# Attention with 32 batches on one core: the context block turned by the vector engine from a second, block-arranged load, instead of by eight transpositions of the tensor engine

## The reference, cut to what matters

```
q  = einsum('oc,bcn->bon', Wq, layernorm(x))        # 512 x 1024 for each batch
k, v = split(einsum('oc,bcn->bon', Wkv, context))   # 512 x 1024 each
q  = softmax(q, over the 64 of a head) * scale
k  = softmax(k, over n)
ctx = einsum('bhdn,bhen->bhde', k, v)               # sum over the 1024 positions n
out = einsum('bhde,bhdn->bhen', ctx, q)
out = Wout @ out + b_out; normalised over its 128 rows; times g
x  = x + out
```

## Time and profile before

| | us |
|---|---|
| median of three runs | 1996.38 |
| the profiled execution | 1997.54 |
| its span | 1995.7 |
| PE busy in the span | 1921.1 (96%) |
| DVE busy | 1381.4 (69%) |
| ACT busy | 1039.4 (52%) |
| POOL busy | 804.2 (40%) |

### The profile page before, as it was taken

How to read it: one execution, slowest core, us unless ns; L and a number is a source line. 1 busy time by engine, 2 the same in 40 slices (tenths; PEclk the granted TensorE clock), 3 DMA queues, 4 the chain that set the end, 5 groups by cost and what they waited for, 6 DMA issues and landing times. The chain is left out here.

```text
span 1995.7 us, 29856 instructions
## 1 busy us (share of the span) xinstructions
PE 1921.1 (96%) x10780; PEld 1662.6 (83%) x10780; DVE 1381.4 (69%) x1985; ACT 1039.4 (52%) x1303; POOL 804.2 (40%) x456
## 2 busy tenths in 40 slices
PE   5999999999999999999998699999999999999999
PEld 4888888888888887878786689999999999999998
DVE  6888888888888888888885744444444455444443
ACT  4787878787878787878785611111111111111111
POOL 4767676767667676767673000000000000000000
PEclk9999999999999999999999799999999999999999
DMA  3111111121212111111111711111111111111110
GB/s 117 54 64 64 63 63 67 59 74 53 74 53 74 53 74 53 74 53 74 53 43 37 221 53 64 64 63 49 46 63 63 63 63 63 63 63 53 44 39 32
DMA packets 43999, 127.64 MB, mean 64 GB/s; under 512 B 4224, under 2 KB 14080, under 8 KB 43968
## 3 DMA queue, kind: packets, MB, share of 16 engines
q1 hardware_dynamic: 39360, 110.44, 15.9%
q0 software_dynamic: 4608, 16.78, 2.7%
HBM read 93.65 MB, written 33.55 MB: 64 GB/s over the span
## 5 line engine op out<-in xcount | busy, mean ns | idle before, releaser
L282 POOL TENSOR_TENSOR kT_lo<-kT,kT_hi 128x1024 fp32r<-128x1024 f32 x128 | 304.6, 2404 | 0.6 <-ACT kT_hi L329 0.5
L278 POOL TENSOR_TENSOR eq<-eq,q_inv 128x1024 f32<-128x1024 f32 x128 | 242.6, 1906 | 140.7 <-DVE q_inv L504 140.7
L966 POOL TENSOR_TENSOR rstd_c<-var_c,minus_half 128x8 f32<-128x8 f32 x32 | 52.8, 1649 | 549.5 <-DVE var_c L1105 549.5
L52 PE MATMUL ps<-w_ra_hi,xT_hi 128*128 128x384 f32 (+1 forms) x768 | 257.3, 335 | 0.0
L54 PE MATMUL ps<-w_ra_hi,xT_lo 128*128 128x384 f32 (+1 forms) x768 | 251.8, 328 | 0.0
L53 PE MATMUL ps<-w_ra_lo,xT_hi 128*128 128x384 f32 (+1 forms) x768 | 251.2, 327 | 0.0
L988 ACT CAST hT_hi<-ps 128x512 fp32r<-128x512 f32 x64 | 37.7, 589 | 375.1 <-PE ps L1162 375.1
L52 PE MATMUL ps<-w_b_hi,hT_hi 128*128 128x512 f32 x512 | 205.4, 401 | 0.0
L347 ACT ACTIVATE ek<-ps,k_min 128x1024 f32<-128x1024 f32 x128 | 142.7, 1114 | 119.6 <-DVE k_min L508 119.5
L54 PE MATMUL ps<-w_b_hi,hT_lo 128*128 128x512 f32 x512 | 200.8, 392 | 0.0
L53 PE MATMUL ps<-w_b_lo,hT_hi 128*128 128x512 f32 x512 | 200.3, 391 | 0.0
(11 more groups left out here) (142 smaller groups left out, 4577.2 us busy)
## 6 DMA issues: line engine op xcount, KB each, us to landing
x_sb<-in_x SPq DMA_DIRECT2D x64, 512.0 KB, 4.1
ctx_hi<-in_ctx POOLq DMA_DIRECT2D x32, 512.0 KB, 3.6
ctx_sb<-in_ctx SPq DMA_DIRECT2D x32, 512.0 KB, 3.3
attention_out<-o_sb SPq DMA_DIRECT2D x32, 512.0 KB, 2.6
o_sb<-attention_out SPq DMA_DIRECT2D x32, 512.0 KB, 3.9
out<-out_sb SPq DMA_DIRECT2D x32, 512.0 KB, 2.9
x<-in_L_ffn_A SPq DMA_DIRECT2D x2, 512.0 KB, 4.0
o_sb<-in_L_ffn_A SPq DMA_DIRECT2D x2, 512.0 KB, 3.7
```

Of the source, the lines that this page charges most:

```text
L52: pe.matmul(out, stat_hi, mov_hi, start=first, stop=False)
L278: pool.tensor_tensor(v, v, per_row(q_inv[:, i, :], 2 * HEADS, DH), ALU.mult).then_inc(q_normed, 1)
L282: pool.tensor_tensor(kT_lo[:, i % 2, :, :], kT[:, i % 2, :, :], kT_hi[:, i % 2, :, :].bitcast(F32), ALU.subtract).then_inc(kT_lo_ready, 1)
```

## The change

The context is read from memory a second time, in sixteen transfers for each batch, into a tile `ctx_blk` whose 32-wide column blocks are arranged so that transposing each 32 x 32 block in place gives the whole transposed context. Each transfer carries a block of 32 rows of the context, of which it takes every fourth run of 32 columns: 32 x 8 runs of 128 bytes. The sixteen stand on SP behind the load of x, and wait until DVE has turned the batch before. DVE transposes all 32 x 32 blocks with one instruction into a tile `cT` in SBUF (no longer in PSUM), between `query_lo(1)` and `max_queries(3)`. ACT's `cT_hi` copy reads `cT` and moves forward, from behind `exp_keys(3)` to before `norm_x`. `cT_lo` moves from DVE to POOL, between `norm_queries` 1 and 2. PE loses its eight transpositions; `RING` loses `C0`, so KT1 of the next step now follows QT2 in its slot. The load of `ctx_sb` no longer waits for the turned context.

```diff
-        "QT0", "K2", "M0", "QT1", "Q3", "QT2", "K3", "QT3", "C0"]
+        "QT0", "K2", "M0", "QT1", "Q3", "QT2", "K3", "QT3"]
...
             def load_context(b, p):
                 wait_for(sp, ctx_lo_ready, b - 1)
-                wait_for(sp, c_turned, b - 1)
                 sp.dma_start(ctx_sb[:, p, :], context[b]).then_inc(ctx_loaded[p], 16)
+
+            def load_blocks(b, p):
+
+                wait_for(sp, c_turned, b)
+                for q in range(P // 32):
+                    dst = ctx_blk[32 * q:32 * q + 32, :].rearrange("p (m c j) -> p m c j", m=NCH, j=32)
+                    for c in range(P // 32):
+                        src = context[b][32 * c:32 * c + 32, :].rearrange("i (m q j) -> i m q j", m=NCH, j=32)
+                        sp.dma_start(dst[:, :, c, :], src[:, :, q, :]).then_inc(blk_loaded[p], 16)
...
+            def context_turned_lo(b):
+                pool.wait_ge(cT_hi_ready, b + 1)
+                pool.tensor_tensor(cT_lo[:, :, :].rearrange("p a b -> p (a b)"), cT[:, :],
+                                   cT_hi[:, :, :].rearrange("p a b -> p (a b)").bitcast(F32),
+                                   ALU.subtract).then_inc(cT_lo_ready, 1)
...
-                act.copy(cT_hi[:, :, :].rearrange("p a b -> p (a b)"), flat("C0")).then_inc(cT_hi_ready, 1)
+                act.copy(cT_hi[:, :, :].rearrange("p a b -> p (a b)"), cT[:, :]).then_inc(cT_hi_ready, 1)
...
+            def turn_context(b, p):
+                dve.wait_ge(blk_loaded[p], 16 * 8 * (b - p) + 256)
+                wait_for(dve, cT_lo_ready, b)
+                dve.transpose(cT[:, :], ctx_blk[:, :]).then_inc(c_turned, 1)
...
-            def turn_context(s, par, edge):
-                wait_slot(pe, "C0", s, edge)
-                pe.wait_ge(ctx_loaded[par], 8 * (s - par) + 16)
-                out = flat("C0")
-                for n in range(NCH):
-                    last = pe.transpose(out[:, n * P:(n + 1) * P], ctx_sb[:, par, n * P:(n + 1) * P], ident[:, :])
-                last.then_inc(c_turned, 1)
```

More of the change, by code:

```diff
@@ L71 @@
 RING = ["KT0", "Q0", "KT1", "K0", "KT2", "Q1", "KT3", "K1", "Q2",
-        "QT0", "K2", "M0", "QT1", "Q3", "QT2", "K3", "QT3", "C0"]
+        "QT0", "K2", "M0", "QT1", "Q3", "QT2", "K3", "QT3"]
 SLOTS = 3
 DELAY = {"X": -1, "K": 0, "C": 0, "Q": 0, "KT": 1, "M": 1, "QT": 1, "O": 2}
-PER_BATCH = {"K": 4, "C": 1, "Q": 4, "KT": 4, "M": 1, "QT": 4}
+PER_BATCH = {"K": 4, "Q": 4, "KT": 4, "M": 1, "QT": 4}
 FIRST_STEP, FULL_FROM, FULL_TO, STEPS = -1, 4, BATCHES - 2, BATCHES + 2
@@ L93, in attention @@
         ctx_sb = sb("ctx_sb", [P, 2, N])
+        ctx_blk = sb("ctx_blk", [P, N])
+        cT = sb("cT", [P, N])
         ctx_hi = sb("ctx_hi", [P, 2, N], F32R)
@@ L140, in attention @@
         ctx_loaded = [sem(f"ctx_loaded{i}") for i in range(2)]
+        blk_loaded = [sem(f"blk_loaded{i}") for i in range(2)]
         x_loaded = [sem(f"x_loaded{i}") for i in range(2)]
@@ L164, in attention @@
         rstd_ready, xn_lo_ready = sem("rstd_ready"), sem("xn_lo_ready")
-        slot_read = {"K": k_exp, "C": cT_lo_ready, "Q": q_shifted, "KT": kT_copied, "M": m_lo_ready,
+        slot_read = {"K": k_exp, "Q": q_shifted, "KT": kT_copied, "M": m_lo_ready,
                      "QT": q_lo_ready}
@@ L190, in wait_slot @@
                 if n < 0:
-                    n, back = n + len(RING), back + 1
+                    n, back = max(m for m in range(len(RING)) if (m - n) % SLOTS == 0), back + 1
                 kind, i = RING[n][:-1], int(RING[n][-1])
@@ L242, in step @@
                     sp.dma_start(o_sb[:, 0, :], o_dram[0]).then_inc(shared["o_loaded"][0], 16)
+                if on("C", s, edge):
+                    load_blocks(s, par)
                 if on("O", s, edge):
@@ L306, in step @@
                     norm_queries(s, par, 1)
+                if C:
+                    context_turned_lo(s)
+                if Q:
                     norm_queries(s, par, 2)
@@ L432, in step @@
                     query_hi(s - 1, 1 - par, 2)
+                if C:
+                    context_turned_hi(s)
                 if X_:
@@ L439, in step @@
                     exp_keys(s, par, 3)
-                if C:
-                    context_turned_hi(s)
                 if Q:
@@ L597, in step @@
                     query_lo(s - 1, 1 - par, 1)
+                if C:
+                    turn_context(s, par)
                 if Q:
@@ L610, in step @@
                     invert_sums(s, 1)
-                if C:
-                    context_turned_lo(s)
                 if Q:
@@ L775, in step @@
                     turn_query(s, par, 3, edge)
-                if C:
-                    turn_context(s, par, edge)
                 if QT:
```

## The result

The changed kernel takes 2087.86 us, the median of four runs (2086.69 to 2090.23), against 1997.27 us for the kernel before, the median of four (1995.07 to 1999.42). The ratio is 1.0455, with a 95% interval of 1.0437 to 1.0473: 4.5% slower. The forecast was 2085, range 2050 to 2132, slower at 0.93.

A forecast was written before the change was run, and what follows sets the result against it. PE was taken as the bound, with a DVE-POOL-PE ring only 0.8 us shorter; 1.13 + 2.38 - 0.75 gave 2.76 us a step, 31 rounds 85.6, with the ends 88, so 2085 us, range 2050 to 2132.

The forecast's parts named there:

- The ring: DVE to POOL to PE and back to `m_lo`: 32.99 us a step, forecast to grow 2.76 to 35.75 us.
- to the start of POOL's first scaling: DVE from `m_lo` through the reciprocal, then handover to POOL: the transposition in this gapless stretch adds 1.13 us.
- POOL's dense stretch: POOL from its first query scaling to the last `kT_lo`, 15.06 us: the inserted `cT_lo` adds its full 2.38 us.
- slack before `add_weighted(3)`: PE's product needing POOL's last `kT_lo`: 0.80 us slack, of which 0.75 is usable and gets used up.
- from there to `m_lo`: From PE's last weighted product through T, folding and ACT to the next `m_lo`: 5.88 us, no addition forecast.
- the first and last rounds: Pipeline ends: the last round pays 0.75 us more, the first pass an estimated 2 us.
- the 0.79 us: PE's eight context transpositions per batch: 25.3 us in all, a gain only while PE binds, otherwise lost in idle time.
- the rival at 1971: Whole attention step: PE stays the bound and its removed transpositions save 25.3 us; chance 0.06.
- PE starts ... without idle time before it: At `add_weighted(3)`, PE's product needing the last `kT_lo`: starts at 621.84 without idling, read as 0.80 us slack.
- Adds nothing to it: ACT's forward copy, 1.0 us later through `exp_keys(3)`: splits PE's waiting, adds none, since the reciprocal moves 1.13 us.
- the estimate of 33 us: Second load's sixteen transfers a batch, if their constants of about 2.0 us added up; issues 0.53 us apart favoured overlap.
- The clock: Rival: PE's granted clock drops for about 3 us of work a step, costing 1.5 us, total 2131; chance 0.07.

The follow-up runs named there:

- e1: The changed kernel with POOL's `cT_lo` subtraction moved before `x_lo`, into idle time; 2031.35 us, ratio 1.0169 to the kernel before.
- e2: The changed kernel with DVE's transposition moved before `folded_lo`, where DVE waits for ACT; 2061.46 us, ratio 1.0322 to the kernel before.
- e6: The changed kernel with PE's eight context transpositions put back into slot `C0`, read by nobody; 2087.59 us, ratio 1.0447 to the kernel before.
- e4: The changed kernel with DVE's transposition, POOL's subtraction and ACT's `cT_hi` copy all moved into idle time; 1996.38 us, ratio 0.9997 to the kernel before.
- e3: The changed kernel with both DVE's transposition and POOL's subtraction moved into idle time; 2031.35 us, ratio 1.0169 to the kernel before.
- e5: The changed kernel without the second load, DVE transposing blocks of `ctx_sb` instead (output not the reference's); 2087.60 us, ratio 1.0448 to the kernel before.

## Why the prediction was right

**The ring.** Its four terms, with forecast and measured change in us: to the start of POOL's first scaling, +1.13 and +1.12 (11.25 to 12.37); POOL's dense stretch, +2.38 and +2.32 (15.06 to 17.38); slack before `add_weighted(3)`, -0.75 and -0.75 (0.80 to 0.05); from there to `m_lo`, 0 and +0.16 (5.88 to 6.04). The sum is 2.85 where 2.76 was forecast, on 32.99. 31 x 2.85 = 88.4 of the 90.9 us between the two profiled executions; 2.5 are left for the first and last rounds, 2.75 were forecast. That these two agree is luck: the first `m_lo` comes 1.44 us later (68.02 against 66.58), where 2 were estimated from no row, and the last round is 4.94 us longer (36.67 against 31.73), where 2.76 + 0.75 were forecast; the granted clock was 0.91 in it. Behind the last `m_lo` 907.0 us follow, against 907.3 before: the expert part is unchanged. e1 and e2 show that both pieces cost by their position: moved into idle time, POOL's gives back 56.5 us and DVE's 26.4.

**PE.** That the 0.79 us lie in idle time was right (e6). The idle time itself is shown as 3.0 us a step, not the forecast 4.2: the profile gives PE 32.82 us of busy time, and the forecast had counted 32.39 - 0.79 = 31.60. But the sentence that 25.3 us are the whole possible gain "while PE is the bound", and the rival at 1971, were wrong. In front of the first key transposition PE was not the bound of the kernel before. With all three pieces in idle time the time is 1996.38, not 1971 (e4). I had found one ring with 0.8 us of slack and taken PE's own work for what fills the step beside it. The reading that failed is "PE starts ... without idle time before it": read at one product, and not at the first key transposition, where the weight loads idled 0.54 us for ACT in each step.

**ACT.** "Adds nothing to it" was right only under cover of POOL's ring. Without this cover the forward move of `cT_hi` costs 2031.35 - 1996.38 = 35 us (e3 against e4): 0.87 us a step on the ring, and 8 us through the clock. The forecast named the cover of DVE's and POOL's pieces, and not this price. It also put 1.8 us of PE idle at the first key transposition; it was 0.91, since PE is held up before that, 0.50 us of it for `shift_queries(3)`, which stands behind the transposition on DVE. Where the transposition is out of the way (e3), it is 1.86.

**The second load.** Hidden, as forecast (e5). The terms were off in both directions and it did not matter: 12.4 ns a packet instead of 37, and 0.74 us an issue instead of 0.53, so that SP's issuing, not the packets, sets the 14 us in which the blocks arrive. The Trainium skill ("DMA: Bandwidth & Descriptors", Anatomy of one DMA) gives a constant of about 2.0 us for a transfer that POOL issues. These are issued by SP, and the trace shows a landing 2.2 us behind the issue in the median, and 2.0 at least. But sixteen of them overlap, so the estimate of 33 us did not come about.

**The clock** was 1.00 in every step of the changed kernel up to the last round, with PE's shown idle time in pieces of at most 1.07 us. So the forecast came out, but its reason, a busy share near 88% and pieces under 2 us, does not hold: in e3 PE is busy 31.5 of 33.86 us with no piece over 1.9 us, and the clock fell in five rounds of 31, at 1.64 us each; in e2, with a piece of 1.89 us, in six. The prediction had put 1.8 us of idle time at just that place; that the changed kernel has only 0.91 there comes from PE's earlier wait for DVE, which the prediction did not see.

## What to carry to other kernels

An engine that is busy 98% of a step need not be what sets it: write down each ring of waits through it, with the slack at every handover, and look at its weight loads too, where a wait of half a microsecond showed that the work in front was free. The price of an added instruction is its place: the same three pieces cost 91 us in dense stretches of two rings and nothing in waits that engines had anyway. And a longer wait of PE can cost more than its own length, when its granted clock falls behind it (8 of the 35 us of e3). A saving on an engine is worth something only after the rings beside it have been shortened: here nothing at first, and then some 15 us.

## What the runs showed that I had not expected

Packets of 128 bytes took 12.4 ns of engine time each, a third of the 37 ns of the mixed small packets at the start of the program. A transfer of this three-part pattern took SP 0.56 us for its own instruction (minimum 563, median 564 ns) and 0.74 us with what stands around it, against 0.33 us for a plain one. The transposition of 128 x 1024 four-byte elements took 1.234 us, like a plain pass over as many; the Trainium skill ("Vector Engine (DVE) Microarchitecture Reference", The reshape front-end and per-opcode configuration) has it sustain one element per cycle and lane, and the trace agrees in so far as the next start is 1.16 us behind, beside 1.13 for a sum over the same elements.
